# An attention and expert kernel on one core: the exponentials' factor as a ScalarE register instead of a column of SBUF

## What is computed

```python
xn = _layernorm(x, axis=-1)
q, k, v = xn @ wq, xn @ wk, xn @ wv            # heads of 16; q, k rotated (rope)
attn = jnp.einsum('bhqd,bhkd->bhqk', q, k) / np.sqrt(HD)
attn = jax.nn.softmax(jnp.where(mask, -jnp.inf, attn), axis=-1)
attention = (attn @ v) @ wo
x1, x3 = ragged_dot(xb, w1b, gs), ragged_dot(xb, w3b, gs)
h = jax.nn.silu(x1) * x3                        # two experts of eight for each token
x = x + attention + experts
```

## Time and profile before

| what | before |
|---|---|
| median of 3 executions | 290.84 us (290.82 to 291.76) |
| span of the profiled execution | 288.9 us |
| median less span | 1.9 us |
| busy PE / DVE / ACT / POOL | 262.5 / 227.5 / 244.4 / 125.8 us |
| PE clock granted, mean | 0.994 |
| exponentials (L543) | 320, busy 182.5 us |

### The profile page before, as it was taken

How to read it: one execution, slowest core, us unless ns; L and a number is a source line. 1 busy time by engine, 2 the same in 40 slices (tenths; PEclk the granted TensorE clock), 3 DMA queues, 4 the chain that set the end, 5 groups by cost and what they waited for, 6 DMA issues and landing times.

```text
span 288.9 us, 6905 instructions
## 1 busy us (share of the span) xinstructions
PE 262.5 (91%) x2307; PEld 115.8 (40%) x2307; DVE 227.5 (79%) x312; ACT 244.4 (85%) x518; POOL 125.8 (44%) x260
## 2 busy tenths in 40 slices
PE   0868599999999999999999998999999999999996
PEld 0534355434344233334343443445523233433454
DVE  3663978999999999998999999995799898033342
ACT  1589876988999999999999998986689989898941
POOL 8386657363458418951135335246005414035020
PEclk9999889999999999999999999999999999999999
DMA  7537074110307103407371001023000300131307
GB/s 238 168 74 138 14 125 110 40 20 2 75 1 111 23 0 77 109 15 120 86 172 41 2 3 37 3 57 73 1 3 16 97 3 0 41 72 19 75 18 166
DMA packets 49106, 17.67 MB, mean 61 GB/s; under 512 B 43120, under 2 KB 48560, under 8 KB 49072
## 3 DMA queue, kind: packets, MB, share of 16 engines
q1 hardware_dynamic: 48384, 16.43, 26.8%
q10 hardware_dynamic: 688, 0.79, 0.8%
HBM read 4.46 MB, written 2.10 MB: 23 GB/s over the span
## 4 chain that ended last, share of the span: by engine, by line
PE 64%; DVE 12%; issue 8%; ACT 6%; POOL 5%; DMA 4%; POOLq 0%; SPq 0%; ACTq 0%
PE ps L808 18%; PE ps L790 13%; DVE PM L657 11%; PE ps L775 10%; PE ps L749 6%; PE ps L827 4%; ACT PR L543 3%; PE ps L848 3%; DMA HT<-HB 3%; PE ps L817 2%; PE ps L767 2%; PE ps L846 2%; PE ps L739 2%; DMA STACKS<-MIXED 1%; PE ps L835 1%
## 5 line engine op out<-in xcount | busy, mean ns | idle before, releaser
L543 ACT ACTIVATE PR<-ps,SCALE 128x512 f32<-128x512 f32 (+1 forms) x320 | 182.5, 654 | 15.7 <-PE ps L790 13.5
L657 DVE TENSOR_REDUCE PM<-ps 128x8 f32<-128x1024 f32 x144 | 167.8, 1218 | 9.0 <-PE ps L775 7.7
L453 POOL TENSOR_SCALAR_AFFINE_SELECT PR<-PR 128x512 f32<-128x512 f32 x64 | 39.8, 635 | 94.7 <-ACT PR L543 94.7
L808 PE MATMUL ps<-PR,VA 128*32 128x512 f32 (+3 forms) x768 | 78.1, 495 | 0.5 <-ACT OA L550 0.5
L790 PE MATMUL ps<-STACKS 64*128 64x512 f16 (+3 forms) x384 | 75.2, 327 | 2.9 <-ACT PR L543 1.4
L775 PE MATMUL ps<-STACKS 64*128 64x128 f16 (+2 forms) x640 | 59.2, 263 | 5.4 <-DVE PM L657 3.7
L790 PEld LDWEIGHTS ps<-STACKS 64*128 64x128 f16 x384 | 24.3, 93 | 57.0 <-ACT PR L543 43.6
L775 PEld LDWEIGHTS ps<-STACKS 64*128 64x128 f16 x640 | 27.1, 95 | 36.7 <-issue 32.1
L468 POOL TENSOR_TENSOR HB<-MIXED,GATE 128x512 bf16<-128x512 f32 x16 | 16.5, 1043 | 30.0 <-DVE MIXED L711 29.6
L808 PEld LDWEIGHTS ps<-PR,VA 128*32 128x32 f32 x768 | 17.0, 108 | 25.9 <-issue 21.1
L749 PE MATMUL ps<-WP,XT 128*128 128x392 f32 x64 | 25.7, 536 | 1.6 <-ACT XT L489 1.6
(11 more groups left out here) (92 smaller groups left out, 234.0 us busy)
## 6 DMA issues: line engine op xcount, KB each, us to landing
X<-x SPq DMA_DIRECT2D x8, 256.0 KB, 6.3
out<-X SPq DMA_DIRECT2D x16, 128.0 KB, 1.9
MIXED<-w SPq DMA_DIRECT2D x3, 512.0 KB, 3.8
STACKS<-MT SPq DMA_DIRECT2D x64, 2.0 KB
WP<-w_proj ACTq DMA_DIRECT2D x1, 392.0 KB, 4.3
WO<-wo ACTq DMA_DIRECT2D x1, 256.0 KB, 6.2
STACKS<-MIXED SPq DMA_TRANSPOSE x16, 3.6
MT<-MPW SPq DMA_TRANSPOSE x16, 2.5
```

The source lines that it names most:

```text
L453: mask = g.affine_select(out=blk, in_=blk, compare_op=ALU.is_ge, fill=0.0, base=0, pattern=[[0, GRP], [1, P]], channel_multiplier=-1)
L543: a.activation(PR[:, k % RING, j, 0:width], bank(step)[:, 0:width], ACT.Exp, scale=SCALE[:]).then_inc(s_exp, 1)
L657: v_.tensor_reduce(spots, two_banks(step).rearrange("p h (a s n) -> p h a s n", a=2, n=P), AX.X, ALU.max).then_inc(m_max, 1)
L808: mm = t_.matmul(o_bank[VW * j:VW * (j + 1), CHUNK - width:CHUNK], VA[:, b * KVH + grp, kb, :], PR[:, n % RING, j, at:at + width], start=i ...
```

## The change

ACT gets a register, `scale_bits`. Once, in the first step `parts` (n is 0), ACT waits until the factor is made and loads the 32 bits of SCALE's first element into the register. Each exponential then names the register as its `scale`, where it named the column of 128 values. The wait for the factor ahead of the first exponential moves to the load. Line numbers below L479 go up by 2, and by 4 behind the load.

```diff
+            scale_bits = a.alloc_register("scale_bits")
+
             for kind, n in steps_of("ACT"):
...
                     if n == 0:
+                        act.wait_ge(scaled, 2)
+                        a.reg_load(scale_bits, SCALE[0:1, 0:1].bitcast(mybir.dt.int32))
                         act.wait_ge(framed, 3)
...
                     act.wait_ge(s_ps, n + 1)
-                    if n == 0:
-                        act.wait_ge(scaled, 2)
 
                     after(act, pv, k - RING + 1)
-                    a.activation(PR[:, k % RING, j, 0:width], bank(step)[:, 0:width], ACT.Exp, scale=SCALE[:]).then_inc(s_exp, 1)
+                    a.activation(PR[:, k % RING, j, 0:width], bank(step)[:, 0:width], ACT.Exp, scale=scale_bits).then_inc(s_exp, 1)
```

## The result

The changed kernel takes 288.85 us (288.14 to 289.27, 4 runs) against 291.23 us (290.82 to 291.76, 4 runs) before, a ratio of 0.991 with an interval of 0.9886 to 0.9933. It is 2.4 us faster, where 6.7 were forecast. The direction held, the size didn't.

The account below looks back on a forecast made before the run. DVE and ACT were taken as full from 55 to 174 us, then PE nearly always busy, ACT full only from 208 to 260. 2.9 + 0.4 + 3.0 + 0.9 = 7.2, less 0.5, gave 284.1 us; range 279.0 to 291.9.

Parts of the forecast that it names:

- The price of the column: On ACT, an exponential without the column saves 0.085 to 0.099 us; 320 take 27 to 32 us less of ACT's time.
- the register costs what the column costs: Rival: exponentials stay at 696 ns and only the load's cost is left, 291.3 us; chance 0.15.
- each register operand adds a step: Rival: a step of 187 ns on ACT before each exponential makes the kernel slower, 305.5 us; chance 0.11.
- The load: One register load on ACT ahead of the first cast of step parts: takes 1.0 us, loses 0.5 at the end.
- The first stage: 55 to 174 us, DVE and ACT both full: saving 2.9 us, capped by DVE's idle time of 4.4.
- 208 to 260 us: 18 score-weight waits, mean 0.55 us, each 0.168 beyond the widest score matmul: saving 3.0 us.
- 174 to 208: 6 score-weight waits, mean 0.45 us, counted only beyond the widest score matmul's 382 ns: saving 0.4 us.
- 260 to 289: 8 score-weight waits of 0.5 us, each 0.118 beyond the widest score matmul: saving 0.9 us.
- the gain is absorbed: Rival: ACT gets faster, but DVE in the first regime and PE in the second absorb it; 289.9 us, chance 0.11.
- the 7.2 us: Sum of the savings over the four stages from 55 to 289 us, before the load's loss; bounds 0 to 17.7.
- the signs that I named: Exponential about 597 ns, ACT 25 us less busy, DVE 97% busy, maxima 3 us sooner, score-weight waits under half of 43.6.
- cheaper yet the score weights still wait as long: Failure condition: exponentials get cheaper, but PE's score-weight loads wait for them as long as before, 43.6 us.

Follow-up runs that it names:

- half exponentials: The register kernel with its load moved into ACT's idle time; exponentials from the twentieth product on compute only half their width: 288.18 us, ratio 0.9887.
- half products: The register kernel, load moved into ACT's idle time; all products but each job's first multiply half their columns: 280.71 us. The same cut with the column: 283.23 us.
- half reductions: Each reduction of the maxima reads half its columns: 280.14 us in the register kernel with its load in ACT's idle time, 288.76 in the kernel before.
- the early load's kernel: The changed kernel with the register load and its wait moved ahead of the third step turned, where ACT idles: 289.27 us, ratio 0.9925.
- the second experiment: The kernel before plus the register load, exponentials keeping the column; the unread register and its load were dropped at build: 291.47 us, ratio 0.9998.
- the literal: The changed kernel without register and load, its exponentials taking the number 8.5 as factor: 288.77 us, ratio 0.9908.
- the load used once: The load where the change has it, its register named by the first exponential alone, the other 319 keeping the column: 291.02 us, ratio 0.9988.
- a second column: The kernel before with a bias column of zeros added to each exponential: 306.01 us, ratio 1.0497.

## Why the prediction was wrong in size

*The price of the column* was right. Forecast were 0.085 to 0.099 us for each exponential; the wide one went from 696 to 600 ns. ACT's busy time fell by 24.0 us all the same, 0.075 for each of 320, and not by 27 to 32. My reading, untested, is that exponentials which wait for scores more often overlap each other less. The rival in which the register costs what the column costs, and the one in which each register operand adds a step, are both out.

*The load* was taken at 1.0 us with a loss of 0.5. It takes 0.52 us and is lost in the 0.53 us of slack that the prediction had found: the loss is nil. Its 0.52 us lie nearer to the lower row, the copy at 0.172, than to the upper at 1.283. The 0.2 us per register of the Trainium skill (Runtime: NRT & Kernel Launch, Instruction fetch mechanics) is also below what the traces show. The page gives it for loads from HBM, and this one reads SBUF; the prediction's conclusion from it, that the slack covers the load, held.

*The first stage*, "I take 2.9", is the first step that failed. The cap of 4.4 us, DVE's idle time, held: 1.7 us were won by 172 us, and 2.2 (172.31 - 170.13, the same copy in the kernel of half exponentials) was all that a much faster ACT won there. But the 2.9 was put down to ACT at second hand: DVE waits for PE, and PE stands behind scores that wait for ACT. Those waits of DVE stayed (7.7 us over the span before [they are 0.8 + 2.1 of rows 6 in this stage], 8.0 after, 7.5 with half exponentials). PE's own work has a share in its being late there: with half products the waits are 5.5 us. What the 1.7 us consist of isn't settled: DVE's idle time in the stage stayed at 4.4 and 4.3 us, in windows that don't hold the same instructions.

*208 to 260 us*, "0.168 beyond the matmul: 3.0 us", is the step that failed most. With the terms of 174 to 208 and 260 to 289 it made 4.3 us, and the measured gain from the 10th to the 16th copy is 0.5. The reading was that a wait of the score weights beyond the length of one matmul is a stall that a faster exponential removes. It isn't: with exponentials of 384 ns in place of 600, 55 waits with 31.6 us remain. The trace of the kernel before has the number that prices it: the score matmuls themselves waited only 0.4 us for exponentials from 208 to 260, and 1.4 in the whole span. The prediction's own rows 7 have 0.6 us for the widest form, and it did not use them. In a fixed order with three banks the weights wait for a bank whenever PE comes by early, and when ACT gets faster PE comes by earlier, until PE's own work fills the time. That is my reading of the counts, 89 waits, then 67, then 55. What is shown is that PE's work counts there: half products shorten the same stretch by 5.9 us, where half reductions shorten it by 2.3 and narrower exponentials by 0.4.

*The rival "the gain is absorbed"* had the mechanism, with DVE and PE as the ones who absorb, and 0.11 of the chances. It supposed that a fifth of the 7.2 us comes through, less 0.5 for the load; a third does, 2.4, and the load costs nothing. The measured gain lay between its 0.9 us and the forecast's 6.7, nearer to the rival. Of the signs that I named, the exponential's duration, the group's busy time (136.6 us) and ACT's longer idle time came, and ACT's busy time fell just short. DVE stayed at 96% in the first stage instead of 97. The last maximum came 1.1 us sooner (its reduction starts at 242.0 for 243.1) instead of 3, or 1.9 (241.2) in the early load's kernel, which has the start of the kernel before, and the waits of the score weights did not fall to under half; "cheaper yet the score weights still wait as long" was named as what would prove the sum wrong.

## What to carry to other kernels

In this kernel a column of equal values as the scale of a 128x512 activation costs about 0.1 us each time; a register that is loaded once costs what an immediate does. But what that is worth is set by the engines beside it: before pricing a saving by the waits for the engine, ask for each stage how much idle time the other full engines have, and take that as the cap of the sum and not as one term. A wait for a buffer in a fixed order isn't a stall to be won back merely because it is longer than the work it lies beside; look first at how long the matmul itself waited, not only its weights, and leave out half of the engine's work once to see if the wait stays.

## What was not expected of the hardware

Equal programs start differently. The first twelve projection matmuls, up to 17 us, took 5.73 us before and 6.21 in its repeat under another name (the second experiment), 6.37 in the changed kernel, 6.28 with the literal, 5.64 with the early load and 6.58 with the load used once. The loads of their weights come 0.65 us apart at first, and closer from some point on that differs by execution. The weights before and after:

```profile
13.55 0.33 PEld L749 LDWEIGHTS ps<-WP,XT 128*128 128x128 f32 x1 [0.32 <-issue]
14.03 1.84 PEld L749 LDWEIGHTS ps<-WP,XT 128*128 128x128 f32 x6 [0.15 <-issue]
```

```profile
14.22 0.34 PEld L751 LDWEIGHTS ps<-WP,XT 128*128 128x128 f32 x1 [0.32 <-issue]
14.87 1.65 PEld L751 LDWEIGHTS ps<-WP,XT 128*128 128x128 f32 x5 [0.32 <-issue]
```

The granted clock reads 1.00, its upper level, over this stretch in each, so the rows don't name the cause. The difference of up to 0.9 us is larger than the load of 0.52 us that I was looking for, and goes through to the first transposes; a single trace would have put it down to the load.

The mean duration misleads on the price of a second column. It is 597 ns without a column (the tanh), 696 with one and 821 with two, steps of 99 and 125. But the distances from start to start, in the sequence of rows 4, here with two columns, say otherwise:

```profile
193.72 2.12 ACT L545 ACTIVATE PR<-ps,ZERO,SCALE 128x512 f32<-128x512 f32 x3
195.71 0.61 ACT L552 COPY OA<-ps 128x512 f32<-128x512 f32 x1
```

(195.71 - 193.72) / 3 = 0.663 us each, 0.093 more than the 0.570 with one column. The closest starts of two wide exponentials in the traces lie 0.48 us apart with the register, 0.57 with one column and 0.66 with two: each column costs the same 0.09.
